# A patch-pooling transformer block on one core: one pooling piece of twelve folded on GpSimd, a re-ordered setup and new engine orders

## Chip, cores and metric

The kernel runs on one core of a Trainium2 chip. The metric is device time in microseconds of one execution. Three executions of the kernel before took 471.18, 472.69 and 472.65 us: the median is 472.65.

## What is computed

`x` is 64 images of 12 channels, 224 x 224, in fp32 (154 MB). Patches of 16 x 16 are summed, mapped from 12 channels to 192 features, and go through one attention and one feed-forward step, each with a layer norm ahead and a residual. All 196 tokens of an image see each other.

```python
pooled = x.reshape(64, 12, 14, 16, 14, 16).sum(axis=(3, 5))
h = einsum('bcij,ce->bije', pooled, channel_weights).reshape(64, 196, 192)
q, k, v = split(layernorm(h) @ W_qkv + b_qkv)
h = h + softmax(q @ k.T / sqrt(192)) @ v
W0, W1, b0, b1 = w_fc * C0, w_proj * C1, b_fc * c0b, b_proj * c1b   # masks mixed from alpha_e, alpha_r
h = h + gelu(layernorm(h) @ W0.T + b0) @ W1.T + b1                  # 192 -> 768 -> 192
```

## The kernel before

A token's feature vector has only 12 degrees of freedom after pooling, so the kernel works on pooled channels and folds the weights into small matrices in a setup: `score_mat` (scores), `g2` (the second norm), `f_stack` (first feed-forward matrix seen from the 25 basis values), `resid_stack`, and W1 as a high and a low fp32r part (`w1_hi`, `w1_lo`).

The images are worked in 16 groups of four. A group's `x` lies on 128 partitions (16 planes, two halves of the image, four runs of four image rows in each patch row) in three tiles `t` of seven rows of patches. `PIECES` cuts a tile into pieces of 2, 2, 2 and 1 patch rows, so a group has 12 slots; slots 3, 7 and 11 are the one-row pieces. There is one buffer `xs` for one group: SyncE's `reload` (L354) waits until VectorE has reduced slot s of group n and then issues the DMAs of slot s of group n + 1, one for each patch row, 448 KB each. So 21 row loads are on their way or waiting to be reduced at any time.

For each group: VectorE's `reduce_piece` (L401, L410) sums 16 x 16 patches in part (what lies on different partitions is summed by TensorE in `sum_rows`, L691). ScalarE copies `p_tok`; VectorE's `norm1`, GpSimd's `root_1` (a power of -0.5) and `scale_p` make the normed channels `phat_tok`. TensorE turns them (`turn_phat`), applies `score_mat` (`apply_a`), and makes the scores twice, once for the row maxima (`scores`, VectorE's `maxima`, L445) and once transposed (`scores_t`) for ScalarE's `exponentials`. `weigh`, `turn_context` and VectorE's `context` (L456) follow; `turn_u`, `apply_g2`, `norm2`, `root_2` and `scale_u` make the second norm. GpSimd splits into high and low parts (`split_u`, `scale_u`). In the feed-forward part TensorE's `hidden` makes 12 units of 128 features, ScalarE's `gelu` writes each twice (L1000 in fp32, L1001 as fp32r `h_hi`), GpSimd's `low_part` subtracts (L1149), and `project` (42 chunks of three matmuls) sums them into seven output tiles. ScalarE's `take_out` copies them out, SyncE's `send` writes them.

Every engine runs one program written out in advance. An iteration n has 72 steps; work of group m with number `now` runs in iteration m + now // 72 at step now % 72. The tables `PE_ORDER`, `ACT_ORDER`, `POOL_ORDER` and `DVE_ORDER` (L93 to L121) give the numbers; at equal steps older groups go first. So the attention of group m runs in iteration m + 1, its feed-forward part in m + 2 and m + 3. Nothing of this changes what an engine waits for, only in which order it comes to it; each engine goes through its own list strictly in order. The `..._SETUP` tables (L123 to L128) place the pieces of the setup as (iteration, step), behind the group work of that step. GpSimd's `setup_wproj` (L1073), at (0, 0), waits for ScalarE's `coef`, which waits for TensorE's; TensorE's `setup_gram` (L623) waits for the centred basis that VectorE's `setup_basis` (L494) makes.

Of the kernel before, what the change touches and what calls it, by code (L numbers as in the profile page):

```python
# [27 lines left out]
ALU = mybir.AluOpType  # L28
# [7 lines left out]
EMBED = 192  # L36
# [44 lines left out]
PAIRED = PAIR_MASK + COLS  # L81

SLOTS = len(PIECES) * TILES
LAG = 3


# [1 line left out]


STEPS = 72  # L90
SEND_SLOTS = (41, 45)

PE_ORDER = {  # L93
    "loop": {
        "sum_rows": (40, 64), "turn_phat": 83, "apply_a": 86, "scores": 90, "turn_max": 100, "scores_t": 103,
        "weigh": 110, "turn_context": 114, "turn_u": 119, "apply_g2": 122, "turn_u_four": 134, "turn_uhat": 146,
        "hidden": (151, 153, 159, 161, 164, 167, 171, 188, 196, 199, 202, 204),
        "project": (183, 185, 187, 189, 190, 192, 193, 195, 197, 198, 200, 201, 203, 205, 207, 209, 210, 216, 217,
            219, 220, 221, 222, 224, 226, 228, 229, 232, 235, 237, 238, 240, 241, 242, 245, 246, 248, 249, 250, 251,
            252, 253),  # L100
    },
}
ACT_ORDER = {
    "loop": {
        "copy_p_tok": 72, "copy_phat": 75, "copy_b": 77, "copy_max": 83, "load_exp": 82, "exponentials": 86,
        "load_gelu": 8, "copy_context": 88, "copy_u": 90, "copy_u_four": 98, "copy_uhat": 145,
        "gelu": (146, 148, 150, 151, 153, 159, 161, 163, 165, 166, 167, 169), "take_out": (168, 228, 229, 236),
    },
}
POOL_ORDER = {  # L110
    "loop": {
        "root_1": 73, "root_2": 88, "scale_p": 74, "scale_u": 89, "p_into_u": 80, "split_u": 86,
        "low_part": (150, 151, 153, 154, 155, 156, 157, 159, 216, 219, 220, 221),
    },
}
DVE_ORDER = {
    "loop": {
        "reduce": (0, 2, 3, 4, 5, 8, 9, 10, 11, 13, 15, 16), "maxima": (78, 79), "context": 84, "norm1": 73,
        "norm2": 86,
    },  # L120
}  # L121

PE_SETUP = {"basis": (0, 0), "coef": (0, 1), "gram": (0, 2), "w1": (0, 71), "w0t": (0, 71), "resid": (1, 14),  # L123
            "f": ((1, 18), (1, 31), (1, 31), (1, 42), (1, 42), (1, 47))}
ACT_SETUP = {"coef": (0, 0), "basis": (0, 1), "w1": (1, 2), "w0t": (1, 2), "f": (1, 18)}
DVE_SETUP = {"gram": (0, 0), "scores": (0, 8), "basis": (0, 8), "g2": (0, 13),
             "biases": (0, 16), "resid": (1, 8), "f": (1, 14)}
POOL_SETUP = {"wproj": (0, 0), "w1": (1, 8), "w0t": (1, 8)}  # L128


def constants():
# [36 lines left out]
def build(nc, x, cw, wqkv, bqkv, wfc, bfc, wproj, bproj, alpha_e, alpha_r, const_full, const_rows, const_paired, out):  # L168
    with ExitStack() as ctx:
# [3 lines left out]
        def sem(name):  # L173
            return ctx.enter_context(nc.semaphore(name))
# [22 lines left out]
        g2 = sb("g2", [128, 128])  # L197
# [6 lines left out]
        xs = sb("xs", [128, TILES, HALF_GRID, RUN * SIDE])  # L204
# [21 lines left out]
        h_f32 = sb("h_f32", [128, 4, COLS_A])  # L226
        h_hi = sb("h_hi", [128, HT, GROUP_TOKENS], F32R)
        h_lo = sb("h_lo", [128, HT, GROUP_TOKENS], F32R)
        out_sb = sb("out_sb", [128, 2, OUT_TILES, EMBED])
# [3 lines left out]
        cwt = prod[0:E2].rearrange("p n h b r -> p (n h b r)")[:, 0:256].rearrange("p (k c) -> p k c", k=2)  # L233
        wfc_sb = out_sb[:, 0, 0:HT, :]
        paired_sb = h_f32[0:COLS].rearrange("p s c -> p (s c)")[:, 0:PAIRED]
        w1_f32 = out_sb[:, 0, 0:HT, :]
        bfc_sb = out_sb[0:1, 1].rearrange("p t e -> p (t e)")[:, 2 * EMBED:2 * EMBED + HIDDEN]
        bproj_sb = out_sb[0:1, 1, 6, :]
        basis_sb, basis_c = out_sb[:, 1, 0, :], out_sb[:, 1, 1, :]
# [18 lines left out]
        setup_pool_self = sem("setup_pool_self")  # L258
        scored = sem("scored")
        reduced = sem("reduced")  # L260
        pool_summed = sem("pool_summed")
        p_tok_ready = sem("p_tok_ready")
        norm1_multiplied = sem("norm1_multiplied")
# [53 lines left out]
        def tile_rows(stack, part):  # L317
            return stack[:, columns[part]].rearrange("p (t m) -> p t m", m=TILE_TOKENS)

        (PE_CWT, PE_G1, PE_ROWS, PE_QKT, PE_A, PE_BASIS, PE_COEF, PE_BT, PE_MIX, PE_G2, PE_W0T, PE_W1, PE_RESID,  # L320
         PE_F) = range(1, 15)
        ACT_CWT, ACT_SEL, ACT_QKT, ACT_COEF, ACT_BT, ACT_W0T, ACT_W1, ACT_FHI = range(1, 9)
        DVE_CWC, DVE_MIX, DVE_GRAM, DVE_SCORE, DVE_CENTRED, DVE_G2, DVE_BIAS, DVE_RESID, DVE_F = (
            3, 5, 6, 7, 11, 12, 13, 14, 15)
        POOL_WPROJ, POOL_W0T, POOL_W1 = range(1, 4)

        block = ctx.enter_context(nc.Block())

# [3 lines left out]
        def order(table, m):  # L332

            return {**table["loop"], **table.get(m, {})}
# [65 lines left out]
        def _(dve):  # L400
            def reduce_piece(n, slot):  # L401

                t, piece = divmod(slot, len(PIECES))
                low, high = PIECES[piece]
                dve.wait_ge(x_landed[slot], 16 * (high - low) * n + 16 * (high - low))
                if piece == 0 and n >= 2:

                    dve.wait_ge(pool_summed, 2 * n - 2)
                rows = xs[:, t, low:high, :].rearrange("p i (r j k) -> p i j r k", r=RUN, k=PATCH)
                dve.tensor_reduce(pooled[n % 2][:, t, GRID * low:GRID * high].rearrange("p (i j) -> p i j", j=GRID), rows,  # L410
                                  AX.XY, ALU.add).then_inc(reduced, 1)

# [475 lines left out]
        def _(act):  # L888
# [19 lines left out]

            def setup_w0t():
                act.wait_ge(setup_pe, PE_W0T)  # L910
                act.copy(w0t[:, :, 0:512], ps[0:E2, 4:6, :])
                act.copy(w0t[:, :, 512:768],
                         ps[0:E2, 6, :].rearrange("p (k c) -> p k c", k=2)).then_inc(setup_act, 1)
# [142 lines left out]
        def _(pool):  # L1056
# [29 lines left out]
            def inverse(part, h):  # L1086
                rows = inv_std[:, part, GROUP * h:GROUP * (h + 1)]
                return rows.unsqueeze(2).broadcast_to([HALF, GROUP, (CHANNELS, BASIS)[part]])

            def root_1(m):  # L1090
                pool.wait_ge(norm1_summed, m + 1)
                if not first(m):

                    pool.wait_ge(phat_tok_ready, 3 * m)
                pool.tensor_tensor(inv_std[:, 0], variance[:, 0], minus_half[:], ALU.pow).then_inc(inv1_ready, 1)  # L1095
# [81 lines left out]
            def iteration(n, on):  # L1177
                for step in range(STEPS):
                    for k in sorted(on, reverse=True):
                        m, now = n - k, STEPS * k + step  # L1180
                        at = order(POOL_ORDER, m)
                        if now == at["root_1"]:
                            root_1(m)
                        if now == at["root_2"]:
                            root_2(m)
                        if now == at["scale_p"]:
                            scale_p(m)
                        if now == at["scale_u"]:
                            scale_u(m)
                        if now == at["p_into_u"]:  # L1190
                            p_into_u(m)
                        if now == at["split_u"]:
                            split_u(m)
                        for unit in range(2 * HT):
                            if now == at["low_part"][unit]:
                                low_part(m, unit)
                    for piece, build_piece in SETUP.items():
                        if is_step(n, POOL_SETUP[piece][0]) and step == POOL_SETUP[piece][1]:
                            build_piece()
# [27 lines left out]
```

## Time and profile before

| | before |
|---|---|
| median of three executions | 472.65 us |
| the profiled execution, its own time | 471.7 us |
| its span in the profile | 469.8 us |
| TensorE matmul, busy | 431.5 us (92%) |
| VectorE, busy | 386.7 us (82%) |
| GpSimd, busy | 345.3 us (73%) |
| ScalarE, busy | 317.4 us (68%) |
| DMA, mean rate over the span | 355 GB/s of 166.72 MB |

PE is TensorE, DVE VectorE, ACT ScalarE, POOL GpSimd and SP SyncE; PEld is the load of weights into TensorE beside its matmuls, and SPq the queue from which SyncE issues DMAs. "Idle before" an instruction is the time its engine stood still ahead of it, with the one that released it behind the arrow. The clock is the share of full speed granted to TensorE. The first 100 us hold the setup and the filling of the pipeline; then iterations of 24.3 us repeat until the last loads land near 415 us; what follows works off the groups still in the pipeline.

### The profile page before, as it was taken

The page shows a single profiled execution, that of the slowest core. Times are in us where ns is not written, and L with a number is a line of the kernel's source. Part 1 is how long each engine was busy: PE and PEld are TensorE (multiplying, and loading weights), DVE is VectorE, ACT ScalarE, POOL GpSimd, SP SyncE. Part 2 cuts the span into 40 slices and gives each one's busy share as a digit, 9 for nine tenths or more (in the row PEclk, how much of TensorE's full clock was granted, in tenths as well). Part 3 has the DMA queues.
Part 4 walks back from the last instruction along what each step waited for, and adds up shares of the span by engine and source line. Part 5 has one row for each costly group of instructions (what it writes and reads, how often), then busy time and mean ns, then how long its engine had stood idle before and what let it go on. Part 6 is the DMA issues. An engine that isn't in the chain of part 4 may idle for free.

```text
span 469.8 us, 10086 instructions
## 1 busy us (share of the span) xinstructions
PE 431.5 (92%) x3794; PEld 373.4 (79%) x3794; DVE 386.7 (82%) x343; ACT 317.4 (68%) x785; POOL 345.3 (73%) x464
## 2 busy tenths in 40 slices
PE   2997795699999999999999999999999999999997
PEld 2745453498989898889898989898989888887897
DVE  3769679899999999999999999999999999941000
ACT  1022325769696868788787878787878786869671
POOL 2014427497979889797979797979797979797981
PEclk9999666699999999999999999999999999999999
DMA  7999999999999999999999999999999999911011
GB/s 242 356 364 405 406 405 405 405 405 405 410 408 407 407 409 409 404 409 406 413 405 412 406 411 407 413 405 409 409 410 409 408 408 407 377 61 31 22 53 53
DMA packets 54026, 166.72 MB, mean 355 GB/s; under 512 B 6031, under 2 KB 6812, under 8 KB 53978
## 3 DMA queue, kind: packets, MB, share of 16 engines
q1 hardware_dynamic: 53978, 166.08, 90.3%
q8 instruction: 30, 0.49, 0.4%
q14 instruction: 18, 0.15, 0.1%
HBM read 156.42 MB, written 9.63 MB: 353 GB/s over the span
## 4 chain that ended last, share of the span: by engine, by line
POOL 32%; PE 32%; ACT 21%; issue 8%; DVE 4%; DMA 1%; SPq 1%; ACTq 0%; DVEq 0%; POOLq 0%
PE ps L567 29%; POOL h_lo L1149 11%; POOL inv_std L1102 5%; ACT probs_t L951 5%; POOL inv_std L1095 4%; ACT L1000 4%; ACT L985 4%; ACT h_f L1000 4%; POOL uhat_four L1125 3%; DVE pooled L410 3%; POOL u_four L1139 3%; ACT h_hi L1001 3%; POOL uhat_tok L1121 2%; POOL phat_tok L1111 1%; POOL uhat_four L1129 1%
## 5 line engine op out<-in xcount | busy, mean ns | idle before, releaser
L410 DVE TENSOR_REDUCE pooled<-xs 128x28 f32<-128x1792 f32 x192 | 331.3, 1777 | 10.7 <-DMA xs<-x 10.6
L1149 POOL TENSOR_TENSOR h_lo<-h_f,h_hi 128x448 fp32r<-128x448 f32 (+1 forms) x192 | 193.2, 1032 | 55.9 <-ACT h_hi L1001 55.7
L567 PE MATMUL ps<-w_hi,h_hi 128*112 128x192 f32 x672 | 186.1, 277 | 0.0
L567 PE MATMUL ps<-w_lo,h_hi 128*112 128x192 f32 x672 | 175.8, 262 | 0.0
L567 PE MATMUL ps<-w_hi,h_lo 128*112 128x192 f32 x672 | 175.7, 261 | 0.0
L567 PEld LDWEIGHTS ps<-w_hi,h_hi 128*112 128x112 f32 x672 | 119.5, 178 | 4.1 <-issue 3.6
L567 PEld LDWEIGHTS ps<-w_lo,h_hi 128*112 128x112 f32 x672 | 119.5, 178 | 1.8
L567 PEld LDWEIGHTS ps<-w_hi,h_lo 128*112 128x112 f32 x672 | 119.9, 178 | 0.0
L1000 ACT ACTIVATE h_f<-ps 128x448 f32<-128x448 f32 (+1 forms) x192 | 97.9, 510 | 25.8 <-PE ps L567 22.2
L1001 ACT ACTIVATE h_hi<-ps 128x448 fp32r<-128x448 f32 (+1 forms) x192 | 97.4, 507 | 0.0
L567 PE MATMUL ps<-uhat_stack,f_stack 128*128 128x448 f32 (+1 forms) x192 | 76.2, 400 | 2.0 <-ACT uhat_stack L968 1.0
L567 PEld LDWEIGHTS ps<-uhat_stack,f_stack 128*128 128x128 f32 x192 | 37.0, 194 | 6.2 <-ACT h_hi L1001 3.6
L445 DVE TENSOR_REDUCE phat_tok<-ps 98x4 f32<-98x784 f32 x32 | 29.7, 971 | 10.8 <-PE ps L567 10.7
L1095 POOL TENSOR_TENSOR inv_std<-variance,minus_half 98x8 f32<-98x8 f32 x16 | 26.4, 1650 | 8.8 <-DVE variance L427 8.8
L1009 ACT COPY out_sb<-ps 112x384 f32<-112x384 f32 x64 | 27.1, 448 | 7.7 <-PE ps L567 7.7
L567 PE MATMUL ps<-resid_stack,u_stack 128*112 128x192 f32 x112 | 31.5, 281 | 0.0
L567 PE MATMUL ps<-sel_gram,pooled 128*98 128x192 f32 x96 | 25.0, 374 | 6.6 <-POOL uhat_four L1129 4.2
L951 ACT ACTIVATE probs_t<-ps 98x392 f32<-98x392 f32 x64 | 26.6, 501 | 6.1 <-PE ps L567 6.1
L966 ACT CAST uhat_stack<-ps 128x392 fp32r<-128x392 f32 x16 | 7.8, 488 | 33.6 <-PE ps L794 33.6
L1102 POOL TENSOR_TENSOR inv_std<-variance,minus_half 98x8 f32<-98x8 f32 x16 | 26.5, 1653 | 1.8 <-DVE variance L439 1.8
L1139 POOL TENSOR_TENSOR u_four<-u_tok,zero 98x200 fp32r<-98x200 f32 x32 | 16.2, 530 | 14.8 <-DVE u_tok L458 14.8
L567 PEld LDWEIGHTS ps<-resid_stack,u_stack 128*112 128x112 f32 x112 | 19.9, 177 | 8.6 <-issue 5.0
(141 smaller groups left out, 537.5 us busy)
## 6 DMA issues: line engine op xcount, KB each, us to landing
xs<-x SPq DMA_DIRECT2D x336, 448.0 KB, 12.6
out<-out_sb SPq DMA_DIRECT2D x16, 336.0 KB, 13.2
out<-out_sb SPq DMA_DIRECT2D x16, 252.0 KB, 13.1
out_sb<-wfc SPq DMA_DIRECT2D x1, 576.0 KB
wproj_sb<-wproj SPq DMA_DIRECT2D x1, 576.0 KB
wqkv_sb<-wqkv SPq DMA_DIRECT2D x1, 432.0 KB
cf<-const_full SPq DMA_DIRECT2D x1, 400.5 KB, 3.3
h_f<-const_paired SPq DMA_DIRECT2D x1, 153.0 KB, 3.6
```

The costliest lines, as they stand in the source:

```text
L410: dve.tensor_reduce(pooled[n % 2][:, t, GRID * low:GRID * high].rearrange("p (i j) -> p i j", j=GRID), rows, AX.XY, ALU.add).then_inc(redu ...
L445: dve.tensor_reduce(phat_tok[:, :, b, MAX_P].rearrange("p h b -> p b h"), ps[0:HALF, b, 0:PAIR_TOKENS].rearrange("p b (h k) -> p b h k", h=2),
L567: return pe.matmul(o, a, b, start=start, stop=stop)
L951: act.activation(probs_t[:, b].rearrange("p k q -> p (k q)"), ps[0:HALF, b, 0:PAIR_TOKENS], ACT.Exp).then_inc(probs_t_ready, 1)
L985: act.activation(warmed[:, 2 * m:2 * m + 1], zero[:], ACT.Exp)
L1000: act.activation(h_f32[:, unit % 4, 0:width[part]], summed, ACT.Gelu_apprx_tanh)
L1001: act.activation(h_hi[:, t, columns[part]], summed, ACT.Gelu_apprx_tanh).then_inc(gelu_done, 1)
L1009: act.copy(out_sb[0:TILE_TOKENS, f % 2, tiles, :], summed[:, 0:tiles.stop - tiles.start, 0:EMBED]).then_inc(out_taken, 1)
L1095: pool.tensor_tensor(inv_std[:, 0], variance[:, 0], minus_half[:], ALU.pow).then_inc(inv1_ready, 1)
L1102: pool.tensor_tensor(inv_std[:, 1], variance[:, 1], minus_half[:], ALU.pow).then_inc(inv2_ready, 1)
L1139: pool.tensor_tensor(high(u_four, h), twice(u_tok[:, h, :, 0:BASIS]), zeros_four, ALU.add).then_inc(u_hi_ready, 1)
L1149: pool.tensor_tensor(h_lo[:, t, columns[part]], h_f32[:, unit % 4, 0:width[part]], h_hi[:, t, columns[part]].bitcast(F32), ALU.subtract).t ...
```

## The change

One slot of twelve, `FOLDED` = 5 (tile 1, patch rows 2 and 3), is halved ahead of VectorE: GpSimd adds, in place, the last two of the four image rows that a partition holds of each patch row onto the first two, and VectorE then sums half as many elements. The queue of row buffers is as before. All four order tables are new; `load_gelu` has the number -124, which no step has. In the setup the W1 part is ahead of the W0 part on all engines, its scratch `w1_f32` lies in `h_f32` and no longer in `out_sb`, and ScalarE's `w0t` has one more wait. The two sends of a group move by two and one slots.

```diff
+FOLDED = 5
-SEND_SLOTS = (41, 45)
+SEND_SLOTS = (39, 44)
...
-        "sum_rows": (40, 64), "turn_phat": 83, "apply_a": 86, "scores": 90, "turn_max": 100, "scores_t": 103,
-        "weigh": 110, "turn_context": 114, "turn_u": 119, "apply_g2": 122, "turn_u_four": 134, "turn_uhat": 146,
+        "sum_rows": (40, 64), "turn_phat": 79, "apply_a": 83, "scores": 87, "turn_max": 95, "scores_t": 100,
+        "weigh": 106, "turn_context": 109, "turn_u": 114, "apply_g2": 118, "turn_u_four": 120, "turn_uhat": 146,
...
-        "copy_p_tok": 72, "copy_phat": 75, "copy_b": 77, "copy_max": 83, "load_exp": 82, "exponentials": 86,
-        "load_gelu": 8, "copy_context": 88, "copy_u": 90, "copy_u_four": 98, "copy_uhat": 145,
-        "gelu": (146, 148, 150, 151, 153, 159, 161, 163, 165, 166, 167, 169), "take_out": (168, 228, 229, 236),
+        "copy_p_tok": 73, "copy_phat": 76, "copy_b": 78, "copy_max": 83, "load_exp": 84, "exponentials": 85,
+        "load_gelu": -124, "copy_context": 87, "copy_u": 89, "copy_u_four": 95, "copy_uhat": 146,
+        "gelu": (149, 151, 152, 153, 154, 160, 162, 165, 166, 168, 170, 216), "take_out": (169, 219, 230, 235),
...
-        "root_1": 73, "root_2": 88, "scale_p": 74, "scale_u": 89, "p_into_u": 80, "split_u": 86,
-        "low_part": (150, 151, 153, 154, 155, 156, 157, 159, 216, 219, 220, 221),
+        "fold": 8, "root_1": 72, "root_2": 89, "scale_p": 73, "scale_u": 90, "p_into_u": 79, "split_u": 85,
+        "low_part": (150, 153, 154, 155, 156, 158, 159, 160, 218, 219, 220, 221),
...
-        "reduce": (0, 2, 3, 4, 5, 8, 9, 10, 11, 13, 15, 16), "maxima": (78, 79), "context": 84, "norm1": 73,
+        "reduce": (0, 2, 3, 4, 7, 8, 9, 10, 12, 13, 15, 16), "maxima": (77, 78), "context": 83, "norm1": 73,
...
-PE_SETUP = {"basis": (0, 0), "coef": (0, 1), "gram": (0, 2), "w1": (0, 71), "w0t": (0, 71), "resid": (1, 14),
-            "f": ((1, 18), (1, 31), (1, 31), (1, 42), (1, 42), (1, 47))}
-ACT_SETUP = {"coef": (0, 0), "basis": (0, 1), "w1": (1, 2), "w0t": (1, 2), "f": (1, 18)}
-DVE_SETUP = {"gram": (0, 0), "scores": (0, 8), "basis": (0, 8), "g2": (0, 13),
-             "biases": (0, 16), "resid": (1, 8), "f": (1, 14)}
-POOL_SETUP = {"wproj": (0, 0), "w1": (1, 8), "w0t": (1, 8)}
+PE_SETUP = {"basis": (0, 0), "coef": (0, 1), "gram": (0, 2), "w1": (0, 3), "w0t": (0, 71), "resid": (1, 15),
+            "f": ((1, 28), (1, 28), (1, 46), (1, 46), (1, 46), (1, 46))}
+ACT_SETUP = {"coef": (0, 0), "basis": (0, 1), "w1": (0, 2), "w0t": (1, 6), "f": (1, 17)}
+DVE_SETUP = {"gram": (0, 0), "scores": (0, 8), "basis": (0, 10), "g2": (0, 13),
+             "biases": (0, 16), "resid": (1, 8), "f": (1, 16)}
+POOL_SETUP = {"wproj": (0, 0), "w1": (0, 9), "w0t": (1, 7)}
...
-                dve.wait_ge(x_landed[slot], 16 * (high - low) * n + 16 * (high - low))
+                if slot == FOLDED:
+                    dve.wait_ge(folded, n + 1)
+                else:
+                    dve.wait_ge(x_landed[slot], 16 * (high - low) * n + 16 * (high - low))
...
+                if slot == FOLDED:
+                    rows = rows[:, :, :, 0:RUN // 2]
...
             def setup_w0t():
                 act.wait_ge(setup_pe, PE_W0T)
+                act.wait_ge(setup_pool, POOL_W1)
...
+            def fold(n):
+
+                t, piece = divmod(FOLDED, len(PIECES))
+                low, high = PIECES[piece]
+                pool.wait_ge(x_landed[FOLDED], 16 * (high - low) * (n + 1))
+                rows = xs[:, t, low:high, :].rearrange("p i (a w) -> p i a w", a=2)
+                pool.tensor_tensor(rows[:, :, 0], rows[:, :, 0], rows[:, :, 1], ALU.add).then_inc(folded, 1)
```

## Rows read from the trace of the kernel before

**Rows 1.** Stretches: us, busy us (instructions) by engine, clock, DMA share, GB/s.

```profile
41.40:74.20 32.80, 25.51 (x121) 16.39 (x121) 25.82 (x28) 10.48 (x23) 14.49 (x18) 0.74 1.03 406
74.20:100.50 26.30, 20.91 (x144) 16.25 (x144) 23.74 (x21) 18.50 (x43) 16.13 (x22) 0.68 1.03 405
219.55:243.81 24.26, 23.53 (x231) 21.29 (x231) 23.67 (x21) 19.10 (x49) 20.77 (x29) 1.00 1.03 408
413.85:438.12 24.27, 23.13 (x227) 20.67 (x227) 5.69 (x10) 19.12 (x48) 20.77 (x30) 1.00 0.10 30
416.00:469.80 53.80, 48.66 (x463) 45.34 (x463) 3.58 (x8) 33.22 (x84) 38.57 (x49) 1.00 0.11 35
```

**Rows 2.** The chain that ended last, steady part: start us, us, what.

```profile
219.55 1.61 POOL inv_std L1102
...
243.81 1.61 POOL inv_std L1102
```

**Rows 3.** Order of time on VectorE, the end: start us, us, instruction, idle before.

```profile
412.95 3.01 DVE L410 TENSOR_REDUCE pooled<-xs 128x28 f32<-128x1792 f32 x2 [0.33 <-DMA xs<-x]
```

**Rows 4.** Order of time on VectorE, the start.

```profile
22.01 2.02 DVE L410 TENSOR_REDUCE pooled<-xs 128x28 f32<-128x1792 f32 x1 [0.26 <-DMA xs<-x]
...
26.97 0.36 DVE L497 COPY out_sb<-ps 128x192 f32<-128x192 f32 x1 [2.42 <-PE ps L567]
...
27.94 0.32 DVE L503 TENSOR_SCALAR out_sb<-out_sb,basis_mean 128x192 f32<-128x192 f32 x1
...
37.32 3.00 DVE L410 TENSOR_REDUCE pooled<-xs 128x28 f32<-128x1792 f32 x2
...
71.12 4.93 DVE L410 TENSOR_REDUCE pooled<-xs 128x28 f32<-128x1792 f32 x3
...
97.48 4.93 DVE L410 TENSOR_REDUCE pooled<-xs 128x28 f32<-128x1792 f32 x3
```

**Rows 5.** Instructions by line and form: busy us, mean ns, idle before.

```profile
L410 DVE TENSOR_REDUCE pooled<-xs 128x28 f32<-128x1792 f32 x144 | 287.1, 2010 | 10.7 <-DMA xs<-x 10.6
...
L1149 POOL TENSOR_TENSOR h_lo<-h_f,h_hi 128x448 fp32r<-128x448 f32 x96 | 108.4, 1152 | 54.6 <-ACT h_hi L1001 54.4
...
L410 DVE TENSOR_REDUCE pooled<-xs 128x14 f32<-128x896 f32 x48 | 51.7, 1076 | 0.0
...
L1084 POOL TENSOR_TENSOR w_lo<-out_sb,w_hi 128x1152 fp32r<-128x1152 f32 x1 | 2.6, 2620 | 0.0
```

**Rows 6.** Order of time on ScalarE and VectorE, the context, steady part.

```profile
238.59 0.33 ACT L956 COPY context_rows<-ps 128x196 f32<-128x196 f32 x1
...
239.43 0.21 DVE L456 RECIPROCAL row_inv<-ps 98x8 f32<-98x8 f32 x1 [0.49 <-PE ps L757]
```

**Rows 7.** Order of time on GpSimd, the start.

```profile
33.72 3.43 POOL L1076 TENSOR_TENSOR wproj_sb<-wproj_sb,probs_t 96x1536 f32<-96x1536 f32 x1 [30.33 <-ACT probs_t L903]
```

**Rows 8.** Order of time on TensorE, the start.

```profile
31.98 0.66 PE L627 MATMUL ps<-cf,out_sb 128*96 128x128 f32 x2
...
35.86 1.22 PE L567 MATMUL ps<-basis_t 96*128 96x128 f32 x4
```

**Rows 9.** Loads of L351 from 96 to 104, and one issue of the page.

```profile
DMA to landing us min/median/max: 7.4/8.9/9.4
...
cf<-const_full SPq DMA_DIRECT2D x1, 400.5 KB, 3.3
```

**Rows 10.** The chain that ended last, its last piece.

```profile
447.77 18.85 PE ps L567 x182
```

**Rows 11.** Order of time on GpSimd, steady part.

```profile
224.77 1.64 POOL L1095 TENSOR_TENSOR inv_std<-variance,minus_half 98x8 f32<-98x8 f32 x1
...
226.98 4.86 POOL L1149 TENSOR_TENSOR h_lo<-h_f,h_hi 128x336 fp32r<-128x336 f32 x5
231.79 0.36 POOL L1172 TENSOR_TENSOR u_tok<-p_tok,zero 98x96 f32<-98x96 f32 x1
...
238.78 2.02 POOL L1149 TENSOR_TENSOR h_lo<-h_f,h_hi 128x448 fp32r<-128x448 f32 x2 [3.33 <-ACT h_hi L1001]
```

More of the change, by code:

```diff
@@ L83 @@
 SLOTS = len(PIECES) * TILES
+FOLDED = 5
 LAG = 3
 STEPS = 72
-SEND_SLOTS = (41, 45)
+SEND_SLOTS = (39, 44)
 PE_ORDER = {
     "loop": {
-        "sum_rows": (40, 64), "turn_phat": 83, "apply_a": 86, "scores": 90, "turn_max": 100, "scores_t": 103,
-        "weigh": 110, "turn_context": 114, "turn_u": 119, "apply_g2": 122, "turn_u_four": 134, "turn_uhat": 146,
[L97 to L100, printed above, removed]
+        "sum_rows": (40, 64), "turn_phat": 79, "apply_a": 83, "scores": 87, "turn_max": 95, "scores_t": 100,
+        "weigh": 106, "turn_context": 109, "turn_u": 114, "apply_g2": 118, "turn_u_four": 120, "turn_uhat": 146,
+        "hidden": (152, 156, 158, 161, 164, 174, 176, 188, 191, 197, 200, 204),
+        "project": (182, 183, 185, 187, 189, 193, 194, 195, 196, 198, 199, 201, 202, 203, 205, 206, 207, 209, 210,
+            216, 217, 219, 220, 221, 222, 225, 226, 229, 232, 234, 235, 237, 238, 240, 241, 242, 243, 245, 247, 249,
+            251, 252),
     },
@@ L235, in build @@
         paired_sb = h_f32[0:COLS].rearrange("p s c -> p (s c)")[:, 0:PAIRED]
-        w1_f32 = out_sb[:, 0, 0:HT, :]
+        w1_f32 = h_f32[:].rearrange("p s c -> p (s c)")[:, 0:HT * EMBED].rearrange("p (t e) -> p t e", t=HT)
         bfc_sb = out_sb[0:1, 1].rearrange("p t e -> p (t e)")[:, 2 * EMBED:2 * EMBED + HIDDEN]
@@ L260, in build @@
         reduced = sem("reduced")
+        folded = sem("folded")
         pool_summed = sem("pool_summed")
@@ L318, in tile_rows @@
             return stack[:, columns[part]].rearrange("p (t m) -> p t m", m=TILE_TOKENS)
-        (PE_CWT, PE_G1, PE_ROWS, PE_QKT, PE_A, PE_BASIS, PE_COEF, PE_BT, PE_MIX, PE_G2, PE_W0T, PE_W1, PE_RESID,
+        (PE_CWT, PE_G1, PE_ROWS, PE_QKT, PE_A, PE_BASIS, PE_COEF, PE_BT, PE_MIX, PE_G2, PE_W1, PE_W0T, PE_RESID,
          PE_F) = range(1, 15)
-        ACT_CWT, ACT_SEL, ACT_QKT, ACT_COEF, ACT_BT, ACT_W0T, ACT_W1, ACT_FHI = range(1, 9)
+        ACT_CWT, ACT_SEL, ACT_QKT, ACT_COEF, ACT_BT, ACT_W1, ACT_W0T, ACT_FHI = range(1, 9)
         DVE_CWC, DVE_MIX, DVE_GRAM, DVE_SCORE, DVE_CENTRED, DVE_G2, DVE_BIAS, DVE_RESID, DVE_F = (
             3, 5, 6, 7, 11, 12, 13, 14, 15)
-        POOL_WPROJ, POOL_W0T, POOL_W1 = range(1, 4)
+        POOL_WPROJ, POOL_W1, POOL_W0T = range(1, 4)
         block = ctx.enter_context(nc.Block())
@@ L1181, in iteration @@
                         at = order(POOL_ORDER, m)
+                        if now == at["fold"]:
+                            fold(m)
                         if now == at["root_1"]:
```

## The prediction, made before the changed kernel ran

> **What bounds the kernel now.** I read the page's slices first: VectorE, TensorE and the DMA engines are all nearly full for most of the span, so shares alone name no bound. The stretches come next [rows 1]; they also show a start of another kind, with a granted clock of 0.74 and 0.68 up to 100.50. One iteration takes 24.26 us at 219.55, with TensorE busy for 23.53, VectorE for 23.67 and GpSimd for 20.77. After the last load, at 413.85, an iteration still takes 24.27 us, although VectorE has only 5.69 us of work left and the DMA engines have a tenth. So the pace is not VectorE's alone. The chain says whose it is [rows 2]: it goes from `root_2` on GpSimd through `root_1`, the attention's matmuls, the exponentials and `low_part` back to `root_2`, once per iteration, with TensorE nearly full beside it. TensorE leaves 24.26 - 23.53 = 0.73 us, and that is all an order can win per iteration.
>
> The second bound is the DMA queue. Its share is 1.03 at 41.40 and in the steady stretch [rows 1]. At the end VectorE waits 0.33 us for a load and ends its last reduction at 412.95 + 3.01 = 415.96 [rows 3]. From 100.49 (97.48 + 3.01, slot 11 of group 2 [rows 4]) this is 315.5 us for 13 iterations, 24.27 each. So compute and DMA finish together: a faster iteration alone can't move the last reduction, since the last load would not have landed. What is behind it, the tail, lasts 53.80 us, of which TensorE works 48.66 [rows 1].
>
> **The fold.** A two-row piece costs VectorE 2,010 ns, a one-row piece of 896 elements 1,076 ns [rows 5]. Slot 5 has half its elements left: 2.01 - 1.08 = 0.93 us less on VectorE per group. GpSimd's nearest rows are 1,152 ns for 448 elements and 2,620 for 1,152 [rows 5]; on the line between them 896 elements take 1.15 + 448 x 2.09 ns = 2.09 us. GpSimd goes from 20.77 to 22.9 us per iteration, VectorE from 23.67 to 22.7. Bounds for the add are 1.15 and 2.62 us; I take 2.1.
>
> What the row shows here is an engine that needs more than twice the time for the same elements (2.09 against 0.93 us). The Trainium skill speaks against the edit: "GPSIMD Engine Reference", section 4.1 (Engine selection), gives elementwise adds to VectorE, since GpSimd takes about twice as long with two inputs. By that rule the add would go to VectorE, where the 448 sums per row cost about what the shorter reduction saves, and nothing would be gained. It is a rule on one instruction's time, though, and here the question is which engine has room.
>
> **The fold's new wait, steady.** `fold` stands at step 8 on GpSimd behind `root_1`, `scale_p`, five `low_part` and `p_into_u`: 2.2 us (224.77 to 226.98) + 4.8 (to 231.79) + 0.36 = 7.4 us [rows 11], so it ends 9.5 us after `root_1` starts. VectorE comes to slot 5 behind `norm1`, three pieces (4.93), two maxima (some 1.9) and slot 4 (2.0), 8.8 us after `norm1`, which ends at or a little ahead of `root_1`'s start. So VectorE will wait about 1 us each time, with slots 5 to 7 and `context` queued behind it. `context` itself needs the exponentials and comes about 13.5 us after `root_1`; slots 5 to 7 need 4.1 us from 9.5. This wait is therefore covered, with nothing to spare. Uncovered it costs up to 1 us an iteration.
>
> **The new orders, steady.** ScalarE copies the context before the fifth GELU; before, it waited behind the table load of GELU and two activations, until 238.59 [rows 6]. `low_part` 8 no longer stands between `scale_u` and `root_1`, 0.9 us of the chain, and the maxima come a piece earlier. Against it, after `context` VectorE now has two pieces instead of one ahead of `norm2` (+2.0 us). Before, `context` came at 239.43 [rows 6], 14.7 us after `root_1` (224.77 [rows 11]); 0.6 us less by the copy and 0.4 to 1.1 by the maxima and by TensorE's waiting make it 13.0 to 13.7. From `context` to the end of the next `norm1` VectorE has 0.5 + two pieces (4.0) + `norm2` 0.7 + slots 10, 11 and 0 (4.9) + 0.5 = 10.6 us. Sum 23.6 to 24.3. `load_gelu` at -124 is never reached: a 0.25 us activation goes from ScalarE, which has 5 us free; its table load is made by the first GELU anyhow. Bounds for an iteration are TensorE's 23.53 and the present 24.27. These ends hold in both directions; I take 23.9, the middle of both pairs.
>
> **The start.** This decides. `fold` of group 0 stands at step 8 of iteration 0; `setup_wproj`, which GpSimd issues at step 0, stands ahead of it and waits for ScalarE's `coef`. Before, it began at 33.72 and took 3.43 us [rows 7]. Everything it waits for is unchanged, so fold 0 runs from 37.15 to 39.25. VectorE reduced slot 5 at 22.01 [rows 4]; it will now stand still until 39.25, and queued behind are slots 6 to 11 and the pieces `scores`, `basis`, `g2` and `biases`. SyncE is held too: it waits for `reduced` before each reload.
>
> Then VectorE needs 1.1 (slot 5) + 0.6 (`scores`, two steps somewhat shorter than the 0.36 of 26.97) + 3.1 (slots 6, 7) + 1.3 (`basis`, 26.97 to 28.26) [rows 4] = 6.1, from 39.3, so TensorE's `gram`, which waits for the centred basis and began at 31.98 [rows 8], begins at 45.4. It took 5.1 us to the end of G2 (31.98 to 35.86 + 1.22 [rows 8]), so `g2` can be made at 50.5. VectorE has done slots 8, 9 by 49.4 and waits 1.1; `g2` 0.3 and slots 10, 11 in 3.0: about 54. Before it was 37.32 + 3.00 = 40.3 [rows 4]. Lag 13.7 us.
>
> Iteration 1 took from 40.3 to 71.12 + 3.01 = 74.1 [rows 4]; of its 32.8 us from 41.40 VectorE worked 25.82 [rows 1], the rest was waiting for attention. Now landed rows wait in the buffers and the setup of W1 is out of the way, made ahead of the attention. With 25.8 - 0.9 of work, 1.3 of biases and 2 to 3 us of waits, slot 11 of group 1 ends near 54 + 29 = 83 (the terms add up to 28.2 to 29.2). Lag 9. The bounds: no waits at all 80.3 (lag 6), all waits kept 87 (lag 13). In iteration 2, 26.30 us with a granted clock of 0.68 [rows 1], the wait ahead of `context` is TensorE's slow half; I expect no gain. Slot 11 of group 2 ends at 109.5 instead of 100.49.
>
> Does the DMA queue run dry? A load issued near 100 took 7.4 us at least to land [rows 9]; `cf`, issued at the start with little ahead of it, took 3.3 [rows 9]. So the cushion there is 4.1 us and the lag 9: the engines idle for 4.9 us, and this is never made up, since the queue is full ever after. The last reduction then ends at 415.96 + 4.9 = 420.9. By compute it is 109.5 + 13 x 23.9 = 420.2. The two again agree; the later one counts, 420.9.
>
> **The rest.** `w1_f32` moves from `out_sb` to `h_f32`; ScalarE's `w0t` waits for GpSimd's W1, long done by then. `basis`, `f`, `resid` and the `take_out` steps move within slack of the start. SEND_SLOTS moves two sends by one or two slots; the sends ahead of the last load are as many as before. All this at zero. In the tail there is no fold. Two chunks of group 13's projection now stand ahead of the last `sum_rows`: six matmuls at 18.85 / 182 = 0.104 us [rows 10], 0.6 us less behind it. The chain's shorter steps give some 0.2 us. Tail 53.0; bounds 48.66 [rows 1] + 3.2 (the drain, 469.8 - 466.62) - 0.6 = 51.3, and 53.8.
>
> **Sum.** 420.9 + 53.0 = 473.9 us of span. The profiled execution took 471.7 against its span of 469.8, 1.9 more, and lies 0.95 below the median of 472.65. So 473.9 + 1.9 + 0.95 = 476.75; I say 476.7.
>
> **Rivals.**
> (1) It comes out faster. Iteration 1 needs no waits and iteration 2 gains from VectorE's shorter work, so that the lag at slot 11 of group 2 is below the cushion of 4.1 us. Then no DMA time is lost, 13 iterations at 23.6 bring compute back to the last load, and the last reduction ends at 416.0. Tail 51.3 to 52.5: span 467.3 to 468.5, time 470.1 to 471.4. For it: VectorE idles some 7 us in iteration 1. Against it: even a lag of 6 exceeds the cushion. 0.15.
> (2) Break-even. Lag near 6, 1.9 us of DMA lost, last reduction at 417.9, tail 53: time 473.7; with the tail's gain 472.5. 0.2.
> (3) The iteration doesn't get shorter: the fold's wait isn't covered, or GpSimd at 22.9 us plus one wait becomes the bound. Then 109.5 + 13 x 24.3 = 425.4, plus 53.8: 479.2, time 482.0; with 24.5 some 3 more. For it: GpSimd waited 3.33 us for the activations every time [rows 11], and that idle time is what the fold fills. A GpSimd add that slowed VectorE's reductions would end here too. Against: shorter chain. 0.2.
> The forecast (474.1 to 479) has 0.45.
>
> The range is 471 to 482: from the top of rival 1 to rival 3. Within 0.3% (about what a measurement of this kernel tells from no change) means 471.2 to 474.1. Rival 1 is faster 0.14, the break-even and a rest of its neighbours 0.21, slower 0.65.
>
> **What would show it.** Right: on VectorE an idle stretch of about 17 us from 22 to 39, released by the fold; `gram` on TensorE near 45.5; slot 11 of group 1 near 83; DMA share under 1 for some us near 100 to 115; iterations of 23.9 with VectorE waits of about 1 us for the fold; last reduction near 421. Wrong: a DMA share of 1.03 throughout with the last reduction at 416 (rival 1), or iterations of 24.3 with TensorE waiting more than 0.73 us in each (rival 3). What would make all of it wrong is a start in which `setup_wproj` runs earlier than 33.7.

## The result, and the profile after

The changed kernel takes 483.33 us, median of four (482.63 to 484.36), against 472.61: a ratio of 1.0235, 95% interval 1.0222 to 1.0249. It is slower, as forecast, but by 10.7 us and not by 4, and it lies above the range of 471 to 482. The profiled execution took 483.62 us, its span is 481.8.

The slices of the page after (busy tenths, the granted clock, DMA share and rate):

```profile
DVE  3507867689898989898989898989898989861000
PEclk9999955559999999999999999999999999999999
DMA  7999998879999999999999999999999999930011
GB/s 245 354 381 405 406 348 320 311 250 368 391 401 410 408 406 409 407 406 407 407 409 409 409 409 407 407 409 406 409 408 410 409 410 409 405 119 30 23 51 51
```

VectorE has an empty third slice, and the DMA rate falls from the sixth slice to the eleventh, to 250 GB/s at the lowest; the kernel before had neither. From slice 12 on the rate is above 400 GB/s again, as before, until the loads end. The granted clock is at half in slices 7 to 10; more on it below. VectorE's order of time over the start:

```profile
19.40 2.02 DVE L417 TENSOR_REDUCE pooled<-xs 128x28 f32<-128x1792 f32 x1 [0.35 <-DMA xs<-x]
39.07 1.09 DVE L417 TENSOR_REDUCE pooled<-xs 128x28 f32<-128x896 f32 x1 [17.65 <-POOL xs L1104]
...
50.20 3.00 DVE L417 TENSOR_REDUCE pooled<-xs 128x28 f32<-128x1792 f32 x2
...
80.72 3.00 DVE L417 TENSOR_REDUCE pooled<-xs 128x28 f32<-128x1792 f32 x2
85.81 1.14 DVE L538 SCALAR_TENSOR_TENSOR f_stack<-u_stack,cf,ps 128x384 fp32r<-128x384 f32 x2 [2.08 <-ACT u_stack L925]
...
106.36 0.21 DVE L463 RECIPROCAL row_inv<-ps 98x8 f32<-98x8 f32 x1 [1.26 <-PE ps L764]
...
112.03 4.93 DVE L417 TENSOR_REDUCE pooled<-xs 128x28 f32<-128x1792 f32 x3
```

The second line is the held start: 17.65 us of idle time, released by the fold (L1104). On GpSimd the cause stands one line ahead of it:

```profile
33.60 3.41 POOL L1084 TENSOR_TENSOR wproj_sb<-wproj_sb,probs_t 96x1536 f32<-96x1536 f32 x1 [30.21 <-ACT probs_t L910]
36.98 2.06 POOL L1104 TENSOR_TENSOR xs<-xs 128x896 f32<-128x896 f32 x1
```

On TensorE `gram` began at 44.86, where it had begun at 31.98 [rows 8]:

```profile
44.86 0.66 PE L634 MATMUL ps<-cf,out_sb 128*96 128x128 f32 x2 [12.92 <-DVE out_sb L510]
```

Stretches (us, busy us by engine, clock, DMA share, GB/s), to be read against [rows 1], and the landing of loads issued from 96 to 104, against [rows 9]:

```profile
60.00:110.00 50.00, 41.32 (x188) 25.41 (x189) 37.62 (x36) 20.25 (x45) 25.18 (x30) 0.50 0.85 311
233.77:257.95 24.18, 23.16 (x231) 20.95 (x230) 22.75 (x21) 19.26 (x47) 22.94 (x30) 1.00 1.03 408
429.60:481.80 52.20, 47.74 (x463) 44.63 (x461) 3.62 (x9) 33.51 (x83) 38.44 (x49) 1.00 0.12 36
```

```profile
DMA to landing us min/median/max: 3.7/4.9/6.7
```

An iteration takes 24.18 us, VectorE is busy for 22.75 of it (23.67 before) and GpSimd for 22.94 (20.77). The last reduction ends at 429.64 (415.96 before), the tail behind it takes 52.2 (53.8). So the span is 12.0 us longer: 13.7 lost in front of the last reduction, less 1.7 gained behind it. VectorE's end, against [rows 3]; it waits for no load:

```profile
426.64 3.00 DVE L417 TENSOR_REDUCE pooled<-xs 128x28 f32<-128x1792 f32 x2
```

The groups of the two reductions and the add, against [rows 5]:

```profile
L417 DVE TENSOR_REDUCE pooled<-xs 128x28 f32<-128x1792 f32 x128 | 254.6, 2009 | 7.6 <-DMA xs<-x 7.6
...
L1104 POOL TENSOR_TENSOR xs<-xs 128x896 f32<-128x896 f32 x16 | 33.8, 2112 | 0.0
```

### The profile page after: what moved, and what is told of

Read it like the earlier page. It is cut to its first block, busy times and chain, and to the rows that moved or that the text cites. A ratio compares the mean times of both kernels' runs of the same rounds, so it can differ in the third digit from the quotient of the medians.

```text
span 481.8 us, 10085 instructions
## 1 busy us (share of the span) xinstructions
PE 430.3 (89%) x3794; PEld 371.1 (77%) x3794; DVE 371.7 (77%) x343; ACT 316.5 (66%) x767; POOL 379.2 (79%) x480
## 4 chain that ended last, share of the span: by engine, by line
PE 47%; POOL 33%; ACT 7%; issue 6%; DVE 4%; DMA 1%; SPq 1%; POOLq 0%; ACTq 0%
PE ps L574 43%; POOL h_lo L1165 6%; ACT probs_t L959 5%; POOL inv_std L1111 5%; POOL inv_std L1118 5%; POOL u_four L1159 3%; POOL u_four L1155 3%; POOL uhat_four L1141 3%; DVE pooled L417 2%; POOL uhat_tok L1137 2%; POOL uhat_four L1145 2%; POOL phat_tok L1127 2%; PE ps L713 1%; DMA xs<-x 1%; PE ps L764 1%
## 5 line engine op out<-in xcount | busy, mean ns | idle before, releaser
L417 DVE TENSOR_REDUCE pooled<-xs 128x28 f32<-128x1792 f32 x192 | 316.2, 1698 | 26.7 <-POOL xs L1104 19.1
L574 PEld LDWEIGHTS ps<-w_hi,h_hi 128*112 128x112 f32 x672 | 119.7, 178 | 17.3 <-issue 11.6
L1017 ACT COPY out_sb<-ps 112x384 f32<-112x384 f32 x64 | 28.7, 448 | 10.1 <-PE ps L574 10.1
L1104 POOL TENSOR_TENSOR xs<-xs 128x896 f32<-128x896 f32 x16 | 33.8, 2112 | 0.0
L574 PE MATMUL ps<-resid_stack,u_stack 128*112 128x192 f32 x112 | 30.5, 272 | 0.0
L1084 POOL TENSOR_TENSOR wproj_sb<-wproj_sb,probs_t 96x1536 f32<-96x1536 f32 x1 | 3.4, 3412 | 30.2 <-ACT probs_t L910 30.2
```

What stands on the lines that cost most here:

```text
L574: return pe.matmul(o, a, b, start=start, stop=stop)
L1017: act.copy(out_sb[0:TILE_TOKENS, f % 2, tiles, :], summed[:, 0:tiles.stop - tiles.start, 0:EMBED]).then_inc(out_taken, 1)
L1104: pool.tensor_tensor(rows[:, :, 0], rows[:, :, 0], rows[:, :, 1], ALU.add).then_inc(folded, 1)
```

## Experiments: the start

The theory: each microsecond for which VectorE is held at the start reaches the end, because the iterations behind it have nothing to give. The rival: the new orders and the new setup lose the time, in iterations 1 and 2 and in the steady part. "The unheld kernel" is from here on the changed kernel with the edit that comes first.

**The hold taken away.** GpSimd's `setup_wproj` stands behind the fold of group 0.

```diff
-POOL_SETUP = {"wproj": (0, 0), ...
+POOL_SETUP = {"wproj": (0, 8), ...
```

> The changed kernel with one number changed: setup_wproj stands at step (0, 8) on GpSimd, behind the fold of group 0, so VectorE isn't held at slot 5 until 39 us. Theory 1 (the held start is nearly the whole loss): slot 11 of group 0 ends near 40 us again, the DMA share stays at 1.03 from 60 to 110 us, and with iterations of 24.2 us the last reduction ends at 416 to 418 and the time is 471 to 473 us. Theory 2 (the new orders lose it, in iteration 2 and in the steady part, whatever the start): 478 us or more. The idle stretch of 17.65 us on VectorE is gone under both.

470.84 us, ratio to before 0.9964 (0.9941 to 0.9986): the kernel is now a little faster than before. One number gives back 12 us, as theory 1 had it. VectorE at the same piece:

```profile
24.02 1.09 DVE L417 TENSOR_REDUCE pooled<-xs 128x28 f32<-128x896 f32 x1 [2.49 <-POOL xs L1104]
```

**The hold alone.** The kernel before, with VectorE waiting for `setup_wproj` ahead of slot 5 of group 0; neither fold nor new orders.

```diff
+                if first(n) and slot == 5:
+                    dve.wait_ge(setup_pool, POOL_WPROJ)
```

> The kernel before with one wait more: VectorE waits for setup_wproj ahead of slot 5 of group 0. No fold, old orders. It prices the held start alone. VectorE stands from 22 to 37 us, slot 11 of group 0 ends near 52 instead of 40.3. Theory 1: most of this lag of 12 us stays to the end (7 to 11 us, 480 to 483 us), since the iterations behind it have 0.7 us each to give. Rival: the waits that VectorE has in iterations 1 and 2 take it up, and the time rises by less than 4 us.

482.76 us, ratio 1.0206 (1.0171 to 1.0241), within the 480 to 483 of theory 1:

```profile
36.93 2.02 DVE L412 TENSOR_REDUCE pooled<-xs 128x28 f32<-128x1792 f32 x1 [15.81 <-POOL wproj_sb L1078]
```

The two runs agree from both sides. The held start takes 17.65 us of waiting, but 2.49 for the fold and 2.81 for a load are there without it too, which leaves 12.35. How the lag travels is seen at `context` (the reciprocal on VectorE) of groups 0, 1 and 2, in us from the span's start:

| | group 0 | group 1 | group 2 | last reduction ends | span |
|---|---|---|---|---|---|
| before | 65.67 | 94.31 | 118.09 | 415.96 | 469.8 |
| before, held | 76.15 | 104.66 | 128.30 | 425.50 | 479.8 |
| changed, not held | 63.63 | 94.21 | 119.55 | 417.70 | 469.9 |
| changed | 75.78 | 106.36 | 131.43 | 429.64 | 481.8 |

The changed kernel lies 12.15, 12.15 and 11.88 us behind the unheld kernel and ends 11.9 behind; the held old kernel lies 10.48, 10.35 and 10.21 behind and ends 10.0 behind. Nothing is taken up on the way, not even by the idle time that VectorE has in iterations 1 and 2. So the rival cannot be the cause of the loss. What is left of it: at group 2 the new orders are 1.5 us behind the old ones, in spite of 2.0 us gained at group 0.

That remainder isn't shown to be the orders' own, for TensorE's granted clock differs too. The stretch from `context` of group 0 to that of group 1 (us, busy us by engine, clock, DMA share, GB/s) in the kernel before, in the changed kernel (the unheld one has 30.58 and 0.50 too), and in two kernels told of below (half of slot 8 left out, and the same with short `low_part`):

```profile
65.67:94.31 28.64, 19.09 (x106) 12.65 (x106) 24.85 (x23) 16.36 (x36) 16.63 (x23) 0.68 1.03 406
75.78:106.36 30.58, 23.57 (x101) 13.40 (x101) 23.91 (x23) 14.05 (x31) 16.55 (x22) 0.50 0.80 284
63.46:90.93 27.47, 18.91 (x101) 10.83 (x100) 22.89 (x22) 14.16 (x31) 16.57 (x22) 0.65 1.03 405
63.33:93.91 30.58, 23.58 (x101) 13.39 (x101) 22.97 (x22) 14.06 (x31) 16.56 (x22) 0.50 1.03 405
```

A clock of 0.50 is the lower of TensorE's two levels, 1.2 GHz; a figure in between is a stretch with both. The last two kernels do the same work in this stretch. Both were at 1.00 up to some 47 us and then at 0.50, with TensorE busy for 10.0 and 10.8 of the 12 us from 48 to 60. Then the first of them was at 1.00 from some 61 to 72 us and the second stayed at 0.50, and the first is 3.1 us shorter. Why only one of them rose no run shows. The ten executions of the kernel without the fold (below) show a step of the same size: the three with a mean clock of 0.960 to 0.964 took 473.8 to 474.4 us, the seven at 0.946 to 0.950 took 476.7 to 478.2. So the 1.9 us by which the stretch is longer than before can be the clock's. The 12 us of the hold can't: the two kernels that differ by the hold alone have the same clock in this stretch, 0.50 and 0.50 in the new orders, 0.68 and 0.68 in the old.

**A shorter hold.** The changed kernel with `FOLDED = 8`, once with `setup_wproj` ahead of the fold and once behind it.

```diff
-FOLDED = 5
+FOLDED = 8
```

> The changed kernel with FOLDED = 8 and setup_wproj ahead of the fold, as in the changed kernel. VectorE is held again, but only from slot 8 on, for some 5 us instead of 17.65, and scores and basis stand ahead of it. If each us of the held start reaches the end (12 of 12 so far), slot 11 of group 0 ends about 5 us later than without the hold and the time is 474 to 476 us. If the end has a threshold (waits that take up the first us), 471 us or less.

Held: 481.08 us, ratio 1.0179 (1.0161 to 1.0196). Unheld, told of below: 477.59 us, ratio 1.01 (1.0079 to 1.0122). `context` of group 0 comes at 67.84 against 64.83, 3.0 us later, group 2 at 123.96 against 120.79, and the span is 3.5 longer. The hold is 6.39 us. The unheld form waits 2.26 us for `g2`, which the held one doesn't; it loses 1.49 us in one `TENSOR_SCALAR` (last section); and its slot 6 began 0.38 us earlier. 6.39 - 2.26 - 1.49 + 0.38 = 3.0. So the hold counts one for one from where it passes what VectorE would have lost anyhow, and the price is read at the first `context`, not at the idle line. My 474 to 476 failed because the unheld form was already at 477.6.

**The setup's f pieces spread** over iteration 1 in the old manner, without the hold.

```diff
-            "f": ((1, 28), (1, 28), (1, 46), (1, 46), (1, 46), (1, 46))}
+            "f": ((1, 23), (1, 28), (1, 28), (1, 37), (1, 37), (1, 42))}
...
-             "biases": (0, 16), "resid": (1, 8), "f": (1, 16)}
+             "biases": (0, 16), "resid": (1, 8), "f": (1, 14)}
```

> setup_wproj behind the fold, FOLDED = 5, and the pieces f spread over TensorE's iteration 1 in the old manner (steps 23, 28, 28, 37, 37, 42) with VectorE's f at step 14 again. It prices the new place of f: in the changed kernel VectorE waited 2.08 us for it behind slot 11 of group 1. If that wait lies on the chain of the start, norm1 of group 1 comes about 2 us earlier (74.6 instead of 76.6) and so does context of group 2; the end gains up to 1.5 us, to the limit of the loads: 469.5 to 470.8. Rival: TensorE's f ahead of the attention's matmuls delays context of group 0 by as much, no change or up to 2 us slower.

473.04 us, ratio 1.0024 (0.9997 to 1.0051): slower than with f at one place (0.9964). The rival of that expectation holds: VectorE then waited 2.49 us for TensorE ahead of `norm2` of group 0, so the wait of 2.08 us had only another place, and its wait ahead of `context` of group 0 grew from 1.86 to 2.99 us (with the fold on slot 8, below, from 2.43 to 3.57). The trace of this kernel is of an execution of 479.6 us, 6 longer than the nine others, with a slower first 40 us, so its stamps aren't compared with those of other kernels.

## Experiments: the iteration

**No fold in the new orders.**

```diff
-FOLDED = 5
+FOLDED = -1
...
-        "fold": 8, ...
+        "fold": -1, ...
```

> The changed kernel without the fold: VectorE sums slot 5 whole, all orders and the new setup kept. The held start is gone too. If the loop that sets the iteration runs through VectorE (13.8 us from root_1 to context, 10.4 from context to root_1), the 0.93 us that slot 5 gets back costs up to 0.93 less the 0.37 us for which VectorE waited ahead of context: iterations of 24.7 to 24.8, the last reduction near 424 and 478 to 480 us. If the fold is no gain in these orders (TensorE or GpSimd set the pace), iterations of 24.2 or less and 471 to 473 us.

477.29 us, ratio 1.0077 (1.005 to 1.0104), a little under the 478 to 480 expected. `context` follows `context` after 24.66 us (144.60 to 169.26), with the fold after 24.18. So in these orders VectorE's work is in the loop, and the fold is worth 0.48 us per iteration. The rest of the 0.93 us is for the most part the 0.37 for which VectorE waited ahead of `context`.

**The fold in the old orders**, without the hold. The kernel before, with `fold`, its wait and the halved slot 5 as in the change, and:

```diff
-        "root_1": 73, "root_2": 88, ...
+        "fold": 8, "root_1": 73, "root_2": 88, ...
-POOL_SETUP = {"wproj": (0, 0), ...
+POOL_SETUP = {"wproj": (0, 8), ...
```

> The kernel before with the fold (GpSimd step 8) and setup_wproj behind it, old orders of all engines and the old setup otherwise. If an iteration is set by the chain through GpSimd, TensorE and ScalarE and the fold lies in the 3.3 us for which GpSimd waited anyhow: 24.3 us per iteration and 472 to 473 us. If VectorE's new wait for the fold counts (GpSimd ends it about 1.8 us after VectorE comes to slot 5; VectorE has 0.93 + 0.49 us to give): 24.6 to 24.7 and 476 to 479 us.

473.23 us, ratio 1.0011 (0.999 to 1.0033); 24.30 us per iteration (24.29 before). The waits from 170 to 340 say why (engine and line, who was waited for: us, times, longest):

```profile
DVE pooled L417 <- POOL xs L1103: 10.6, 7, 1.5
```

VectorE waits 1.5 us for the fold in each of seven iterations: the 0.93 it saved and the 0.49 it used to wait for `context` [rows 6]. The fold alone gains nothing, the orders alone lose 0.37 us per iteration (24.66), the two together gain 0.1.

**The add left out**, in the unheld kernel. No fold on GpSimd, and VectorE still sums only half of slot 5, so half of that piece is missing from the sums.

```diff
-        "fold": 8, ...
+        "fold": -1, ...
-                if slot == FOLDED:
-                    dve.wait_ge(folded, n + 1)
-                else:
+                if True:
                     dve.wait_ge(x_landed[slot], 16 * (high - low) * n + 16 * (high - low))
```

> The same kernel with the GpSimd add left out: VectorE sums half of slot 5, the other half is missing from the sums. It prices the add on GpSimd. Theory: the add lies ahead of a wait for u_tok (0.69 us per iteration in the steady part) and ends before VectorE comes to slot 5, so up to 1.4 us of it push others; low_part 1 to 4 come 2.1 us earlier, but nobody who waits for them sets the pace: iterations of 24.1 to 24.2, time 469.5 to 471. Rival: the add or its contention with VectorE costs the iteration, which then falls to 23.8 or less.

471.33 us, ratio 0.9967 (0.9948 to 0.9986), 24.17 us per iteration. With the add it was 0.9964. GpSimd's 2.1 us cost nothing in the new orders: GpSimd now waits 2.8 us for `u_tok`, where it waited 0.7. Against the kernel without the fold (24.66) only VectorE's half reduction differs, so the 0.48 us are its worth alone.

```profile
POOL u_four L1153 <- DVE u_tok L463: 19.5, 7, 2.8
```

**Half of slot 8 left out of the sums**, in the unheld kernel, and then **half the columns of `low_part` 5 to 7 left out** as well.

```diff
-                if slot == FOLDED:
+                if slot in (FOLDED, 8):
                     rows = rows[:, :, :, 0:RUN // 2]
```

```diff
...
+                w = width[part] if first(f) or unit not in (5, 6, 7) else width[part] // 2
...
```

> The kernel with setup_wproj behind the fold, and VectorE sums only half of slot 8 without a fold (half of that piece is left out of the sums). It takes 0.93 us from VectorE behind context and nothing from GpSimd. Two loops share root_1 to context (13.8 us): back through VectorE 10.4 us, back through GpSimd (split_u, three low_part, root_2, scale_u) 10.0. Theory: 24.18 goes to 23.8 and not to 23.25, because GpSimd's loop is only 0.39 us shorter. Rival: VectorE alone sets it, 23.3; or TensorE does, 24.2. Measured on the middle iterations; the end is held by the loads, 469 to 470.5 us.

> As the run with half of slot 8, and low_part 5 to 7 subtract only half of their columns from group 1 on (the rest of the low parts is left out), which takes some 1.4 us from GpSimd between u_tok and root_2. If GpSimd's loop is the second one, the iteration falls from 23.8 to 23.3 to 23.5, near TensorE's 23.2 of work. Rival: no change against the run with half of slot 8.

The iteration falls to 23.76 us with the first (`context` at 211.24 and 235.01) and to 23.25 with both (212.21 and 235.46). VectorE's 0.93 us less give 0.42, and 1.2 us less on GpSimd (three `low_part` in 1.69 us instead of 2.91; 1.4 had been expected) give another 0.51. So two loops lie nearly on top of each other. Both run from `root_1` to `context`; one returns through VectorE's pieces, the other through `split_u`, three `low_part`, `root_2` and `scale_u` on GpSimd. `root_1` itself shows which of them comes last: in the unheld kernel, with half of slot 8 left out, and with the short `low_part` as well,

```profile
226.69 1.65 POOL L1111 TENSOR_TENSOR inv_std<-variance,minus_half 98x8 f32<-98x8 f32 x1 [0.38 <-DVE variance L434]
...
221.21 1.66 POOL L1111 TENSOR_TENSOR inv_std<-variance,minus_half 98x8 f32<-98x8 f32 x1
...
221.69 1.65 POOL L1111 TENSOR_TENSOR inv_std<-variance,minus_half 98x8 f32<-98x8 f32 x1 [0.69 <-DVE variance L434]
```

In the first GpSimd waits 0.38 us for VectorE's `norm1`, so its own loop is that much shorter; in the second it comes last itself; in the third it waits for VectorE again, and 0.51 + 0.69 is the 1.2 us taken from it. That is why less work on VectorE alone buys no more than 0.4 us. Less work on GpSimd alone was not run; from the wait of 0.38 us it should buy nothing.

And yet the times are 471.4 us (0.9974, 0.9952 to 0.9995) and 469.25 (0.9943, 0.9921 to 0.9965). 13 iterations at 23.76 would have brought the last reduction to 412. It ended at 416.15 and 416.85, since compute had caught up with the loads (the 469 to 470.5 us expected of the first left too little for that). In the first of the two, from 320 to 416,

```profile
DVE pooled L417 <- DMA xs<-x: 4.3, 4, 1.8
DVE pooled L417 <- POOL xs L1104: 4.0, 4, 1.1
```

and four of its last iterations take 24.9 to 26.0 us (in the second one takes 27.2). This is the second bound of the prediction: without a hold it lies at 416 to 417.

**The fold on slot 8**, unheld (the first diff below); the same with f spread, by the diff above; and the fold on slot 8 at step 12 of GpSimd (the second diff on top of the first).

```diff
-FOLDED = 5
+FOLDED = 8
...
-POOL_SETUP = {"wproj": (0, 0), ...
+POOL_SETUP = {"wproj": (0, 8), ...
```

```diff
-        "fold": 8, ...
+        "fold": 12, ...
...
-POOL_SETUP = {"wproj": (0, 8), "w1": (0, 9), ...
+POOL_SETUP = {"wproj": (0, 12), "w1": (0, 13), ...
```

> setup_wproj behind the fold as in the run before, and FOLDED = 8 in place of 5. Slot 8 stands behind context on VectorE, where it never waits; slot 5 stands ahead of it, where VectorE waited 0.37 us. If the loop through VectorE sets the iteration, the whole 0.93 us count behind context and 0.93 - 0.37 = 0.56 come back ahead of it: 24.18 - 0.37 = 23.8 us per iteration. The last reduction can't end before about 416 us for the loads, so only 1 to 2 us of the 5 reach the end: 469 to 470.5 us. Rival: TensorE or GpSimd set the iteration, and it stays at 24.2 with 470.8 us.

> Both: FOLDED = 8 and f spread, setup_wproj behind the fold. With iterations of 23.8 us and an earlier start compute is ahead of the loads by some us, and VectorE waits for loads over the last iterations. If the loads are the bound, the last reduction ends at 415 to 417 us as with either edit alone and the time is that of the better of the two within 0.5 us (469 to 470.5). If the loads are no bound, both gains add up: 466 to 467 us.

> FOLDED = 8 with the fold at step 12 of GpSimd in place of 8 (setup_wproj and W1 moved behind it). With the fold at step 8, GpSimd stood 2.85, 2.43 and 1.88 us for the load of slot 8 in the last three iterations. Four low_part later (4.4 us) the load has landed: theory, all iterations take 24.2 us and the time is that of the fold of slot 5, 470 to 472. Rival: slot 8 is no place for a fold even without that wait, 475 or more. In iteration 0 GpSimd holds W1 no longer than before.

477.59 us (1.01, 1.0079 to 1.0122), 479.23 (1.0149, 1.0127 to 1.0171) and 472.78 (0.9999, 0.9981 to 1.0018). The first expectation failed twice. The iteration stayed at 24.24 and did not fall to 23.8: `context` now comes 0.5 us later behind the whole slot 5, and the loop through GpSimd has only 0.4 us of room. And the end grew longer. GpSimd from 340 to 420:

```profile
359.24 2.11 POOL L1104 TENSOR_TENSOR xs<-xs 128x896 f32<-128x896 f32 x1 [2.85 <-DMA xs<-x]
384.70 2.11 POOL L1104 TENSOR_TENSOR xs<-xs 128x896 f32<-128x896 f32 x1 [2.43 <-DMA xs<-x]
409.63 2.11 POOL L1104 TENSOR_TENSOR xs<-xs 128x896 f32<-128x896 f32 x1 [1.88 <-DMA xs<-x]
```

As compute draws near the loads, the fold waits for slot 8 in the middle of GpSimd's list, with four `low_part` and `split_u` queued behind, and `context` follows `context` after 25.9 and 25.5 us. Four `low_part` later the load has landed: 24.2 us to the last. This fold is still 1.9 us slower than that of slot 5 (470.84) and misses the 470 to 472 expected; 1.4 of it is there at `context` of group 0 already (65.04 against 63.63), where a `TENSOR_SCALAR` beside the fold takes 1.47 us longer (last section). With f spread it was slower still, as in the run above, and not 469 to 470.5 as expected.

## Why the prediction came out too low

**Right, and nearly to the number.** The hold (fold from 36.98 to 39.04; forecast 37.15 to 39.25), `gram` at 44.86 (45.4), slot 11 of group 0 at 53.2 (54), slot 11 of group 1 at 83.7 (83); the add, 2.11 us (2.09), and VectorE's 22.75 (22.7). Two runs show that this hold is the whole loss. The loads ran dry as said, though from 60 us on and not only near 100: those issued near 100 landed after 3.7 us at the least (median 4.9), close to the 3.3 that had been taken as the floor from the first issue.

**The step that failed: "Iteration 1 took ... Lag 9", and with it "I expect no gain. Slot 11 of group 2 ends at 109.5".** The lag was to fall from 13.7 to 9 us in iteration 1, as idle time took it up, and then to stay. Nothing of the hold was taken up: against the unheld kernel it is 12.15, 12.15 and 11.88 us at `context` of groups 0 to 2, since the idle time was waiting for a chain which the hold had delayed as well. Slot 11 of group 2 ended at 112.03 + 3.0 = 115.0, 5.5 us later than forecast and 14.5 later than before: 11.9 of these are the hold; the other 2.7 the unheld kernel has too (100.15 + 3.0 = 103.15 there, against 100.49), and the prediction put them at nothing.

That slot 11 of group 1 came out right is luck of the marker. At `context`, where all engines meet, the lag against before is 10.1, 12.1 and 13.3 us for groups 0 to 2; at slot 11 it reads 12.9, 9.6 and 14.5. The change puts one piece more between `context` and slot 11, and in iteration 1 it moves VectorE's f from ahead of slot 11 to behind it. In iteration 1 the two nearly cancel (7.9 us from `context` to the end of slot 11, before 8.5); in iteration 2, with no f, the piece stands alone (8.7, before 6.2).

**The second term, mis-sized: an iteration of 23.9.** It took 24.18 to 24.2; over 13 iterations 3.8 us. The sum of 23.6 to 24.3 held the value, and the middle was chosen without a reason. TensorE's 0.73 us of idle time were taken as what an order can win, with its 23.53 us of work as the bound; in the changed kernel it works 23.16 and stands idle for 1.0. The runs show two loops, through VectorE and through GpSimd, that set the pace; with both made shorter an iteration took 23.25. The forecast wait of 1 us for the fold did not come: VectorE waits 0.96 us ahead of the maxima instead, and so reaches slot 5 after the fold has ended.

**The loads.** They were said to hold the last reduction to 420.9. They lost more than the forecast 4.9 us: 311 GB/s in place of 405 from 60 to 110 us is 50 x 94 / 405 = 11.6 us. They still weren't the last, since compute was later yet, at 109.5 + 5.5 + 13 x 24.2 = 429.6. The idea of a floor was right, and two experiments end on it (416 to 417 unheld).

**The tail** took 52.2 us, forecast 53.0. Together: 473.9 + 8.7 - 0.8 = 481.8, the span. Rival 3, at 482.0, was the nearest, but by luck: its iterations of 24.3 nearly came true, its wait for the fold did not, and it starts from the same 109.5.

## What to carry to other kernels

An instruction that is free in every iteration can be dear in the first one: look at what stands ahead of it in its engine's list at the start, above all a setup piece that waits for other engines. A lag is measured where the engines meet and where no edit moved the marker; idle time of an engine doesn't absorb it when it waits for the same chain. Before work is moved to the engine with room, ask which loops have nearly the same length, and what bound (here the loads) lies just behind them: here an edit on VectorE alone gave 0.4 us per iteration, and both together, with work left out, 3 us in all (469.25 against 472.31).

## What was not expected of the hardware

In four kernels one instruction of the setup on VectorE, a `TENSOR_SCALAR` over 128 x 192 fp32 from SBUF to SBUF, took many times its 0.32 us [rows 4]. They are those in which GpSimd was at work when it started; in the ten others it took 0.32. In the kernel with f spread, VectorE and GpSimd:

```profile
35.54 3.13 DVE L510 TENSOR_SCALAR out_sb<-out_sb,basis_mean 128x192 f32<-128x192 f32 x1
```

```profile
35.13 3.42 POOL L1084 TENSOR_TENSOR wproj_sb<-wproj_sb,probs_t 96x1536 f32<-96x1536 f32 x1 [8.97 <-ACT probs_t L910]
```

It ends 0.1 us after GpSimd's product ends (38.67 and 38.55), and in the three kernels with the fold on slot 8 unheld it took 1.79 to 1.81 us and ended 0.12 after the fold. The pooling reductions beside the fold did not change: 2,009 ns with it, 2,010 without [rows 5]. The Trainium skill, "GPSIMD Engine Reference", section 8 (Key points), says that the two engines share their way into SBUF and that VectorE contends when its instruction works in a two-port mode or has two SBUF inputs; which mode this instruction ran in no run here shows. That reductions with their one input stayed free agrees with it. That the one instruction waits until the other has ended fits all four traces, but was not tried by itself.
